# A condition loaded once a batch, and waits moved into the arms of the branch

## The reference

```python
x = rotate(x, theta[b], phi[b])                     # pairs of features
x = layernorm(x + gelu(x @ Wi[e] + bi[e]) @ Wo[e] + bo[e]) # e = itok_B_0_7[b], one of 8 experts
out = {0: gelu(x @ w1_nr) @ w2_nr,                  # c = itok_B_0_2[b] chooses
       1: gelu(x @ w1_tsr) @ w2_tsr,
       2: gelu(gelu(x @ w1_sr) @ w2_sr) @ w3_sr}[c] # biases left out here
x = layernorm(x + out) * gamma + beta
x = adaptive_layernorm(x, itok_B_34_63[b])
x = x + attention(x, fside[b], mask[b]) @ Wo        # 16 heads, a 256 x 256 bias each
x = x + gelu2(layernorm(x) @ W1) @ W2
```

## Time and profile before

| What | Value |
|---|---|
| median of 3 runs | 2076.05 us (2075.35 to 2077.53) |
| span of the profiled execution | 2069.5 us |
| the profiled execution's own time, by that span and the median | 2076.05 us, 6.5 us around the span |
| PE busy | 1921.3 us, 93% |
| DVE busy | 1590.7 us, 77% |
| ACT busy | 1376.7 us, 67% |
| POOL busy | 252.4 us, 12% |
| DMA queue q1, share of 16 engines | 56.0% |
| granted TensorE clock, mean | 0.985 |

### The profile page before, as it was taken

One profiled execution on the slowest core, in us unless ns is written; L12 is line 12 of the kernel. 1 busy time (PEld: TensorE's weight loads), 2 busy tenths in 40 slices (PEclk: granted clock), 3 DMA queues, 4 the chain that ended last, 5 costly groups with the idle time before them and its releaser, 6 DMA issues.

```text
span 2069.5 us, 43614 instructions
## 1 busy us (share of the span) xinstructions
PE 1921.3 (93%) x14354; PEld 1676.1 (81%) x14354; DVE 1590.7 (77%) x5373; ACT 1376.7 (67%) x2210; POOL 252.4 (12%) x361
## 2 busy tenths in 40 slices
PE   5789999999999999999999999999999999999786
PEld 4668888888888888888888888888888888788676
DVE  4577877787887788887777888778888877877774
ACT  3376677677667677767767767766776776666443
POOL 1111111011111011111001111101111110111100
PEclk9799999999999999999999999999999999999998
DMA  6655555665565566654555655556665546653450
GB/s 221 202 172 167 187 153 158 186 203 182 183 178 148 156 202 192 196 181 154 154 187 183 195 172 179 164 174 201 189 196 181 177 146 177 216 159 118 133 153 11
DMA packets 222311, 356.12 MB, mean 172 GB/s; under 512 B 29523, under 2 KB 120147, under 8 KB 222068
## 3 DMA queue, kind: packets, MB, share of 16 engines
q1 hardware_dynamic: 222068, 352.99, 56.0%
HBM read 294.12 MB, written 58.79 MB: 171 GB/s over the span
## 4 chain that ended last, share of the span: by engine, by line
PE 76%; DVE 12%; issue 5%; ACT 4%; DMA 1%; ACTq 0%; SPq 0%; POOL 0%; DVEq 0%; POOLq 0%
PE pD L471 51%; PE pX L687 11%; PE pS L471 9%; DVE bias_ring L1178 4%; PE pC L471 3%; DVE bias_ring L975 3%; PE pC L709 1%; DVE x_nat L972 1%; ACT L777 1%; DVE crossed L972 1%; ACT gelu_out L777 1%; ACT probs L777 1%; ACT hid L777 1%; DVE res L978 0%; DVE y_nat L978 0%
## 5 line engine op out<-in xcount | busy, mean ns | idle before, releaser
L1178 DVE CUSTOM_DVE_ANT_0 bias_ring<-pS,bias_ring 128x256 f32<-128x256 f32 x1024 | 389.5, 418 | 200.3 <-PE pS L471 197.4
L777 ACT ACTIVATE probs<-pX 128x512 f32<-128x512 f32 x512 | 304.6, 595 | 225.1 <-PE pX L687 222.8
L777 ACT ACT_TABLE_LOAD x341 | 437.5, 1283 | 18.9 <-PE pD L471 12.0
L687 PE MATMUL pX<-ident,bias_ring 128*128 128x128 f32 x2048 | 321.2, 280 | 61.4 <-DVE bias_ring L975 49.3
L687 PEld LDWEIGHTS pX<-ident,bias_ring 128*128 128x128 f32 x2048 | 228.9, 141 | 147.2 <-issue 95.9
L975 DVE TENSOR_SCALAR bias_ring<-bias_ring,row_max 128x256 f32<-128x256 f32 x1024 | 321.8, 357 | 18.3
L471 PE MATMUL pS<-k_stack,q_stack 96*128 96x256 f32 x1024 | 304.5, 379 | 0.0
L471 PE MATMUL pD<-x,raw 128*128 128x256 f32 x1024 | 246.4, 384 | 3.0 <-ACT gelu_out L777 1.0
L471 PE MATMUL pD<-raw,gelu_out 128*128 128x256 f32 x1024 | 237.6, 379 | 0.0
L471 PEld LDWEIGHTS pS<-k_stack,q_stack 96*128 96x128 f32 x1024 | 197.9, 193 | 19.8
L471 PEld LDWEIGHTS pD<-x,raw 128*128 128x128 f32 x1024 | 188.2, 191 | 31.8 <-issue 9.7
(11 more groups left out here) (148 smaller groups left out, 3663.4 us busy)
## 6 DMA issues: line engine op xcount, KB each, us to landing
bias_ring<-in_fside SPq DMA_DIRECT2D x512, 256.0 KB, 4.4
raw<-in_experts SPq DMA_DIRECT2D x128, 512.0 KB, 4.7
q_spill<-hid SPq DMA_DIRECT2D x96, 256.0 KB, 3.4
k_spill<-hid SPq DMA_DIRECT2D x96, 256.0 KB, 3.4
q_stack<-q_spill SPq DMA_DIRECT2D x128, 192.0 KB, 4.3
k_stack<-k_spill SPq DMA_DIRECT2D x64, 384.0 KB, 5.6
norm<-in_expert_rows SPq DMA_DIRECT2D x32, 384.0 KB, 4.1
x_nat<-in_x SPq DMA_DIRECT2D x32, 256.0 KB, 3.1
```

Source lines behind the costliest of these rows:

```text
L687: last = e.transpose(pX[:, k, t * P:(t + 1) * P], bias_ring[:, u % NBIAS, t, k * P:(k + 1) * P], ident[:, :])
L777: return e.activation(o, i, func, bias=bias, scale=scale)
L1178: e.tensor_tensor_reduce(bias_ring[:, n, t, :], pS[:, t, :], bias_ring[:, n, t, :], 1.0, -3.4e38, ALU.add, ALU.max, row_max[:, n, t:t + 1] ...
```

## The change

On each of the three engines, c is loaded once a batch, at the very start of `front(b)`'s first step, that is in front of the step that stands before the branch: on PE in front of the waits for the transposes of y_nat, on ACT in front of the waits for xa_hi, on DVE in front of the wait for x1_hi. The register is used by all later compares of the batch. The waits that stood in front of the compares stand inside the arms, as the first thing that an arm does: x1_hi in three arms of `branch_in`, the three waits of the narrow arms of `branch_out` (helper `narrow_ready`), `branch_seeded` in its deep arm, and ACT's waits for the hidden tile (helper `hid_free`) in its two arms. SP's own loads of c are as before.

```diff
             def front(b):
                 def branch_in():
-                    low = sem["x1_lo"], b + 1
-                    e.wait_ge(sem["x1_hi"], b + 1)
-                    c = e.value_load(idx[0:1, 1, b:b + 1])
+                    high, low = (sem["x1_hi"], b + 1), (sem["x1_lo"], b + 1)
                     with e.If(c == 2):
+                        e.wait_ge(*high)
                         for i in range(2):
                             to_turned(BANK[f"deep{i}"], "w1_sr", SR, 2 * P * i, xa, low).then_inc(sem["pe_deep"], 1)
                     with e.Else():
                         with e.If(c == 1):
+                            e.wait_ge(*high)
                             to_turned(BANK["narrow"], "w1_tsr", H, 0, xa, low).then_inc(sem["pe_narrow"], 1)
                         with e.Else():
+                            e.wait_ge(*high)
                             to_turned(BANK["narrow"], "w1_nr", H, 0, xa, low).then_inc(sem["pe_narrow"], 1)
                 def branch_middle():
-                    c = e.value_load(idx[0:1, 1, b:b + 1])
                     with e.If(c == 2):
...
                 def branch_out():
-                    e.wait_ge(sem["branch_seeded"], b + 1)
-                    c = e.value_load(idx[0:1, 1, b:b + 1])
+
+                    def narrow_ready():
+                        e.wait_ge(sem["branch_seeded"], b + 1)
+                        e.wait_ge(sem["act_narrow"], 3 * b + 3)
+                        e.wait_ge(sem["dve_narrow"], b + 1)
+
                     with e.If(c == 2):
+                        e.wait_ge(sem["branch_seeded"], b + 1)
                         e.wait_ge(sem["act_deep"], 9 * b + 9)
...
                     with e.Else():
-                        e.wait_ge(sem["act_narrow"], 3 * b + 3)
-                        e.wait_ge(sem["dve_narrow"], b + 1)
                         with e.If(c == 1):
+                            narrow_ready()
...
                         with e.Else():
+                            narrow_ready()
...
+                c = e.value_load(idx[0:1, 1, b:b + 1])
                 if b:
                     e.wait_ge(sem["v_made"], 2 * b)
                 e.wait_ge(sem["y1_made"], b + 1)
@@ ACT, front(b)
+                c = e.value_load(idx[0:1, 1, b:b + 1])
                 e.wait_ge(sem["y1_turned"], b + 1)
                 if b:
                     e.wait_ge(sem["branch_done"], b)
                 act(flat(xa_hi[:, :, :]), flat(pD[:, BANK["y1"], :, :]), ACT.Copy).then_inc(sem["x1_hi"], 1)
                 yield
-                if b:
-                    e.wait_ge(sem["dma_spill"], 96 * b)
-                e.wait_ge(sem["wide_out"], 4 * b + 4)
-                if not b:
-                    e.wait_ge(sem["dve_cols"], 1)
-                c = e.value_load(idx[0:1, 1, b:b + 1])
+                def hid_free():
+                    if b:
+                        e.wait_ge(sem["dma_spill"], 96 * b)
+                    e.wait_ge(sem["wide_out"], 4 * b + 4)
+                    if not b:
+                        e.wait_ge(sem["dve_cols"], 1)
+
                 with e.If(c == 2):
+                    hid_free()
                     deep(0)
                     deep(1)
                 with e.Else():
+                    hid_free()
                     narrow()
...
-                c = e.value_load(idx[0:1, 1, b:b + 1])
                 with e.If(c == 2):
```

## The result

The changed kernel takes 2078.36 us (median of 20 runs, 2076.61 to 2082.65) against 2074.66 (20 runs, 2066.16 to 2078.29): ratio 1.0023, 95% interval 1.0015 to 1.003. That is 5 us slower (3 to 6), where I had forecast 18 us faster. The profiled execution has a span of 2075.1 us; the one before had 2069.5.

The account below looks back on a forecast made before the run. The order of work on PE was taken as the bound (busy 93%). 15.2 + 3.0 + 0.7 + 0.3 = 19.2, less some 1 us for slow compares, gave 18 us: time 2058, range 2052 to 2069.

Parts of the forecast that it names:

- (6): ACT's loads L847, L859 and DVE's loads run beside their engines' work: zero each; only the last batch may give 0.3 us.
- Does what follows let it pass?: After the input branch's arm: the 0.89 us wait before ACT's gated has room, so PE's whole shift reaches gated and scores.
- (1): Input branch, PE: load leaves, compares run before x1_hi; of 17.2 us idle in 25 batches, 15.2 go once ACT's delay is counted.
- (2): ACT's load in front of xa_hi: xa_hi and x1_hi come about 0.12 us later per batch, bounds 0 and 0.31.
- rival B: ACT's load costs nothing, because the sequencer runs it during ctx_raw's wait: 3 us more gain, 2055 us; chance 0.09.
- (3): branch_middle, PE: load L608 goes, but the matmuls in front hide the sequencer; worth nothing except in the last batch.
- (4): branch_out, PE: 2.9 us of issue won't pass, 6.4 us waiting for hid stays; taken as 0, last batch 0.7 us.
- (5): PE's load in front of y_nat's transposes: hidden by score matmuls, free by a small margin; otherwise at most 12 us in all.
- A: Rival: PE's compares get no head start before x1_hi, only the load is saved: 8 us, time 2068; chance 0.15.
- E: Rival: branch_out's 2.9 us pass too, and the startup's idle: 2052 us; chance 0.04.
- C: Rival: PE gains 18 us but a downstream wait on DVE or ACT ends when it did: about 2074 us; chance 0.08.
- D: Rival: slower; ACT's load falls wholly on x1_hi, PE has no head start, compares take longer: 2082 us; chance 0.06.

## Why the prediction was wrong

The parts, each measured alone or worked out from two runs:

| part | forecast, us | measured alone, us |
|---|---|---|
| TensorE's branch_in (15.2 + 3.0, and the 3.0 of ScalarE's delay, which has a row of its own here) | -21.2 | -22 (17 with the load at y_nat, and the 5 of the third row; with the load behind branch_out 21 were measured) |
| ScalarE's load ahead of xa_hi (0.12 in 25 batches) | +3.0 | +2 |
| TensorE's load ahead of y_nat | 0, at most 12 | +5 |
| ScalarE's waits inside the arms | not in the sum | +16 (on before), +18 (on the changed kernel) |
| sum | -18 | +1 to +3; the whole change measured +5 (3 to 6) |

The forecast's 0.7 and 0.3 us for the last batch and its 1 us for slow compares cancel and are left out. The 2 to 4 us between the sum and the whole change are no more than the rows' intervals, of 2 to 3 us to either side each.

**The step that failed is (6), on ScalarE**, and with it the paragraph "Does what follows let it pass?". Step (6) costs ScalarE's two loads of c at zero in their own place and says nothing of its waits, although the diff moves dma_spill and wide_out from in front of the branch into the arm: a term put at nothing without a reason, which measured 16 to 18 us. The waits themselves are satisfied. What they change is where the wait for TensorE's result stands: not on gelu any more but ahead of the table load, so that 42.1 us instead of 12.0 are waited there. I had also read "gelu waited only 0.20 for PE" as ScalarE being nearly late, and so reckoned that "The 0.89 in front of gated has room". The timeline had the table load of 1.28 us in the row above that gelu. It was never asked what let it start early.

The trace of the kernel before could have told it. There `deep(2)` waits for dve_deep and then for pe_deep, two waits, and its table load stands waiting, where the one of `deep(0)`, with a single wait inside the arm, in the same batch does not:
```profile
1121.67 1.28 ACT L777 ACT_TABLE_LOAD   x1
...
1131.03 1.28 ACT L777 ACT_TABLE_LOAD   x1 [1.30 <-PE pD L471]
```
Nine such waits make the 12.0 us that the table loads waited for TensorE before. They stand in every kernel here; whether the other order of those two waits would give some of it back was not tried.

**(1) Right.** The compares run ahead: one of L596 starts at 1427.4 (0.21 us), and xa_hi ends at 1427.56 + 0.60 = 1428.16, and the first matmul follows 0.05 us later, at 1428.21. In 31 of the 32 batches the first compare starts before xa_hi ends, mostly 0.55 us before, and the arm's first weight load comes 0.05 us after xa_hi in the median.
```profile
L596 PEldq COMPARE_BRANCH  x1: 207/207/207, 1427.4 to 1427.4; - x1
```
**(2) Right in mechanism and about in size.** Over the 26 batches in which ctx_raw is right in front of xa_hi, xa_hi starts 0.39 us behind it in the median, before 0.28: 0.11 us, where I had 0.12. In the batch shown it was 0.56, since the load took 0.46 there:
```profile
L843 ACTq TENSOR_LOAD <-idx x1: 457/457/457, 1427.0 to 1427.0; - x1
```
It starts with ctx_raw, not in the 0.20 us in which ctx_raw waited; in all 26 batches it starts 0.01 us after ctx_raw does, which had waited 0.20 us or more. So rival B, and with it the rule of the Trainium skill ("Perfetto Trace Analysis", "DVE / Act Engine Instruction") that the sequencer is free once an instruction waits in the queue, doesn't hold at this place; the 2 us of that load alone (0.4 to 4.4) say the same.

**(3) and (4) not refuted, but (4) misread a term.** I had written that the 6.4 us of waiting for hid stay and that at most the 2.9 of issue go. In the window it came out the other way about:
```profile
L471 PEld LDWEIGHTS pD<-w_hi,hid 128*128 128x128 f32 x200 | 32.6, 190 | 6.9 <-issue 6.9
```
No wait for hid stands there any more, 6.9 us are issue, and the total fell from 9.7 to 6.9 (19.5 to 13.9 over the whole run). Part of that may be the same waiting under another name, now that more waits stand in the arm; no run tells. What it is worth in time is not shown either: the kernels with and without the parts at branch_middle and branch_out differ by -3.5 us in one comparison and by +1.8 in the other (which has VectorE's loads moved too), neither outside its interval. x_nat's transposes wait in 27 places instead of 20, 21.4 us instead of 20.3.

**(5) Wrong in size, inside its bounds.** The margin was counted with a load of 0.30 us, the duration in each of the 32 rows of L597 but the first. In its new place the load takes 0.50 in the median and up to 0.84 us:
```profile
L637 PEldq TENSOR_LOAD <-idx x32: 297/495/844, 29.8 to 1921.5; - x32
```
The cover in front holds a load of 0.30 us, as I had reckoned: between 320 and 1500 us the loads of 0.30 to 0.33 us leave no idle time in front of y_nat. Those of 0.74 to 0.84 leave 0.3 to 0.4 us.

**(6), the rest, right.** VectorE's new load takes up to 0.86 us, and xa_lo still starts 0.03 us after xa_hi in most batches, as before.

**The rivals.** A and B did not occur: the compares have their head start, and xa_hi is later. Of E, branch_out's 2.9 us, the runs leave open how much passes. C named the right symptom, a gain given back in a wait downstream on ScalarE, without its cause. D had the right sign and a wrong cause: TensorE kept its head start. It put 0.40 us a batch on ScalarE's load, some 13 us over 32 batches; that load alone measured 2. (The chances given add to 0.86 for faster and 0.08 for same, where I wrote 0.87 and 0.07.) Of the signs I named, gelu's wait for PE is gone, as forecast, but only because it moved to the table load one row up; gated no longer waits in 25 batches (93 waits in all instead of 118):
```profile
ACT gated L783 <- PE pD L471: 87.5, 93, 3.2
```
That was among my signs for "wrong", as was the new hole in front of y_nat, and it is the one to look at first.

With ScalarE's waits back in front of the branch or in the other order, the rest of the change gives 2059.92 or 2061.47 us, 2 to 4 above the forecast 2058. So the sum was sound for most of the parts that it held; the 5 us of the load ahead of y_nat, which it had at zero, are more than what is missing.

## What to carry to other kernels

When a wait moves, ask what the compiled program puts between it and the instruction that it is meant for. In the programs here the first of several waits keeps the place on the instruction, even when it is always satisfied, and the others stand ahead of the table load. So on ScalarE the wait that really waits should come first, or the others should stay in front of the branch, so that a table load can run under it. A long instruction that shows no wait in the profile is cover that can be lost: price it as you price a stall. And a register load hoisted away from a wait should land where the queued work in front is longer than the load at its slowest, not at its median: look for another engine's load at the same instant to see how slow it can be there.

## What the runs showed that I had not expected

A register load from SBUF takes 0.27 to 0.31 us in most places, and up to 0.9 us in front of y_nat. The trace of the kernel before had slow ones already: SyncE's load of c for the branch's bias row, at line 336.
```profile
L336 SPq TENSOR_LOAD <-idx x32: 267/649/906, 12.7 to 1907.6; - x32
```
In the changed kernel 17 of TensorE's 20 loads over 0.35 us ran beside that load of SyncE, and so did 3 of its 12 shorter ones. Which of the two slows the other, or whether something slows both, the runs don't tell; SyncE's was slow before TensorE's stood there.

Here are stretches of the changed kernel that each are one such load of TensorE (the last two numbers: DMA share, GB/s):
```profile
442.33:443.13 0.80, 0.79 (x6) 0.55 (x5) 0.42 (x1) 0.80 (x3) 0.00 (x0) 1.00 1.06 388
1121.38:1122.22 0.84, 0.78 (x6) 0.54 (x5) 0.44 (x2) 0.84 (x3) 0.00 (x0) 1.00 1.02 371
...
501.88:502.20 0.32, 0.32 (x5) 0.31 (x4) 0.32 (x1) 0.32 (x2) 0.00 (x0) 1.00 0.07 22
...
813.78:814.10 0.32, 0.32 (x5) 0.31 (x4) 0.32 (x1) 0.32 (x2) 0.00 (x0) 1.00 1.02 375
```
The two loads of 0.8 us ran while the DMA engines were full; of those of 0.3 us one ran while they were nearly idle, and one while they were full. So full DMA engines go with the slow loads but don't make one by themselves. What does was not tried, and is open.
